# Feed-forward of a decoder layer: gate weights as the stationary operand, routes of all rows computed first, latent product ahead of the down projection

## The reference

```python
def _L0_ffn_ref(hidden_states, gate_w, up_w, down_w, fc1_w, fc2_w, expert_w, ln_gamma, ln_beta):
    HID, INT, LAT, NE, K = (512, 1024, 256, 8, 2)
    logits = jnp.einsum('bsh,he->bse', hidden_states, gate_w)
    routing_weights, selected_experts = jax.lax.top_k(logits, K)
    h = jax.nn.relu(jnp.einsum('bsh,hi->bsi', hidden_states, up_w)) ** 2
    shared_out = jnp.einsum('bsi,ih->bsh', h, down_w)
    x_latent = jnp.einsum('bsh,hl->bsl', hidden_states, fc1_w)
    expert_out = jnp.einsum('bsl,lm->bsm', x_latent, expert_w)
    moe_out = expert_out * jnp.sum(routing_weights, axis=-1, keepdims=True)
    routed_out = jnp.einsum('bsl,lh->bsh', moe_out, fc2_w)
    return _layernorm(shared_out + routed_out, ln_gamma, ln_beta)
...
x = _layernorm(x + _L0_ffn_ref(x, ...), axis=-1)
```

## Time and profile before

| | |
|---|---|
| median of 3 runs | 889.41 us (888.95 to 889.97) |
| profiled execution, its own time | 889.44 us |
| its span, first to last instruction | 887.3 us |
| PE busy | 858.8 us, 97% of the span |
| DVE busy | 608.7 us, 69% |
| POOL busy | 454.6 us, 51% |
| ACT busy | 424.6 us, 48% |
| mean granted TensorE clock | 0.995 of full speed |

### The profile page before, as it was taken

One profiled execution on the slowest core, in us unless ns is written; L12 is line 12 of the kernel. 1 busy time (PEld: TensorE's weight loads), 2 busy tenths in 40 slices (PEclk: granted clock), 3 DMA queues, 4 the chain that ended last, 5 costly groups with the idle time before them and its releaser, 6 DMA issues.

```text
span 887.3 us, 15395 instructions
## 1 busy us (share of the span) xinstructions
PE 858.8 (97%) x4780; PEld 714.8 (81%) x4780; DVE 608.7 (69%) x2043; ACT 424.6 (48%) x1430; POOL 454.6 (51%) x406
## 2 busy tenths in 40 slices
PE   7999999999999999999999999999999999999995
PEld 5787788788877788888888888888888877787884
DVE  5466788888877766666666666666667667556645
ACT  4345877777761544444444444444444455430310
POOL 4625866766674544444444444444444569471002
PEclk9999999999999999999999999999999999999998
DMA  8679998867763111213112113121131122000000
GB/s 277 263 225 214 211 184 165 184 146 159 158 233 139 39 34 35 107 37 107 37 36 108 36 37 108 36 78 66 37 107 37 48 72 85 25 11 36 13 13 35
DMA packets 68368, 88.23 MB, mean 99 GB/s; under 512 B 7232, under 2 KB 44352, under 8 KB 67264
## 3 DMA queue, kind: packets, MB, share of 16 engines
q1 hardware_dynamic: 68288, 87.26, 35.8%
HBM read 64.13 MB, written 23.07 MB: 98 GB/s over the span
## 4 chain that ended last, share of the span: by engine, by line
PE 83%; POOL 5%; DVE 4%; issue 3%; ACT 3%; DMA 1%; SPq 1%; POOLq 0%; ACTq 0%; DVEq 0%
PE banks L35 68%; PE banks L1096 6%; PE banks L1078 3%; PE banks L738 3%; PE banks L756 1%; PE banks L729 1%; POOL B_wv L171 1%; POOL x L1626 1%; PE banks L122 1%; ACT B_prob L667 1%; SPq L213 1%; POOL B_prob L579 1%; DMA heads_k<-heads_k_d 0%; DVE B_prob L824 0%; DMA stage<-xT_dram 0%
## 5 line engine op out<-in xcount | busy, mean ns | idle before, releaser
L35 PE MATMUL banks<-C_wo,C_o 128*128 128x512 f32 x768 | 192.3, 399 | 1.3 <-issue 1.2
L35 PE MATMUL banks<-xT,C_w 128*128 128x512 f32 x768 | 185.7, 390 | 0.8 <-DVE xT L137 0.8
L35 PEld LDWEIGHTS banks<-xT,C_w 128*128 128x128 f32 x768 | 143.6, 188 | 31.1 <-issue 1.6
L35 PEld LDWEIGHTS banks<-C_wo,C_o 128*128 128x128 f32 x768 | 139.6, 188 | 29.4 <-ACT C_o L1037 1.6
L1037 ACT ACTIVATE C_o<-banks 128x512 fp32r<-128x512 f32 x64 | 38.3, 598 | 231.3 <-PE banks L35 231.3
L667 ACT ACTIVATE B_prob<-B_prob,B_top 128x128 f32<-128x128 f32 x256 | 99.5, 393 | 26.4 <-DVE B_top L824 26.2
L1021 ACT ACTIVATE C_prob<-C_prob,C_top 128x128 f32<-128x128 f32 x256 | 99.0, 391 | 8.4 <-DVE C_top L1162 8.4
L171 POOL TENSOR_TENSOR C_wo<-stage,C_wo 128x512 fp32r<-128x512 f32 x32 | 40.9, 1277 | 110.6 <-ACT C_wo L166 110.6
L171 POOL TENSOR_TENSOR C_w<-stage,C_w 128x512 fp32r<-128x512 f32 x32 | 40.8, 1277 | 105.5 <-ACT C_w L166 105.4
L1224 POOL TENSOR_TENSOR C_q<-C_t,C_t 128x512 f32<-128x512 f32 x64 | 82.9, 1295 | 13.1 <-DVE C_t L1149 13.1
L579 POOL TENSOR_TENSOR B_prob<-B_prob,B_rden 128x512 f32<-128x512 f32 x64 | 67.5, 1057 | 37.0 <-DVE B_rden L833 36.6
(11 more groups left out here) (141 smaller groups left out, 1657.8 us busy)
## 6 DMA issues: line engine op xcount, KB each, us to landing
C_kv<-cross_kv_d SPq DMA_DIRECT2D x8, 1536.0 KB, 6.9
cross_kv_d<-B_v_out SPq DMA_DIRECT2D x16, 512.0 KB, 4.2
stage<-wq_dram SPq DMA_DIRECT2D x32, 256.0 KB, 2.6
stage<-wo_dram SPq DMA_DIRECT2D x32, 256.0 KB, 2.6
heads_q<-heads_q_d SPq DMA_DIRECT2D x96, 64.0 KB, 3.8
heads_k<-heads_k_d SPq DMA_DIRECT2D x96, 64.0 KB, 3.9
heads_q_d<-cT SPq DMA_DIRECT2D x8, 512.0 KB, 2.9
heads_k_d<-cT SPq DMA_DIRECT2D x8, 512.0 KB, 2.8
```

The source lines that it names most:

```text
L35: mm = eng.matmul(out, stationary[i], moving[j], start=first and n == 0, stop=last and n == len(PASSES) - 1)
```

## The change

Four edits, all in the feed-forward.

1. The gate product is turned round: `ghl` (16 or 8 columns) is stationary and the turned x moves, 512 tokens at a time, so 16 matmuls of 512 columns for all rows (`gates`), whose result has the experts on partitions. They stand on PE behind the eighth tile of half 0 (`GATES = 6`). ACT copies the two results to SBUF (`copy_gates`, in front of its work for the next tile). Behind the last tile of half 0, 8 small float32 matmuls (`turn_gates`) turn them back, 128 tokens each, and add the two parts by a 16x8 matrix of two identities (`fold`).
2. The routes of all 8 rows are made at once on DVE (`routes`), ahead of row 0.
3. Within a row, the latent product comes first; ACT copies it out, scaled by the route (`D_routed`), and z is then the down product (from PSUM) plus that.
4. In each half the order of tiles is up 0 to 5, fc1 0 and 1, up 6 and 7.

```diff
-    tiles = [("lat", l, 0) for l in range(L)] + \
-            [("up", m, 0) for m in range(M)] + [("fc1", l, 0) for l in range(L)] + \
-            [("up", m, 1) for m in range(M)] + [("fc1", l, 1) for l in range(L)]
+    GATES = 6
+
+    order = [("up", m) for m in range(6)] + [("fc1", 0), ("fc1", 1), ("up", 6), ("up", 7)]
+    tiles = [("lat", 0, 0), ("lat", 1, 0)] + [(kind, m, 0) for kind, m in order] + [(kind, m, 1) for kind, m in order]
...
+        self.gT = pool("gT", 104, [P, 2, D])
...
-        self.glo, self.logit = chip.small("D_glo", [P, self.E]), chip.small("D_logit", [P, self.E])
-        self.best, self.route = chip.small("D_best", [P, self.E]), chip.small("D_route", [P, 1])
+        self.fold, self.logit = chip.small("D_fold", [P, self.E]), chip.small("D_logit", [P, B, self.E])
+        self.best, self.route = chip.small("D_best", [P, B, self.E]), chip.small("D_route", [P, B])
...
-        self.dn, self.rt, self.gt = [chip.bank(2), chip.bank(5)], chip.bank(3), chip.bank(4)
+        self.dn, self.rt = [chip.bank(2), chip.bank(5)], chip.bank(3)
+        self.gt, self.tg = [chip.bank(4), chip.bank(3)], chip.bank(5)
...
     def scalar_rows(self, eng, b):
 
-        eng.wait_ge(self.s_gt, b + 1)
-        wait(eng, self.s_logit, b)
-        eng.activation(self.glo[:, :], self.gt[:, self.E:2 * self.E], ACT.Copy).then_inc(self.s_gcopy, 1)
-        eng.wait_ge(self.s_dn, b + 1)
+        eng.wait_ge(self.s_rt, b + 1)
+        eng.wait_ge(self.s_route, 1)
         wait(eng, self.s_z, b)
-        eng.activation(self.shared[:, :], self.dn[b % 2], ACT.Copy).then_inc(self.s_shared, 1)
+        eng.activation(self.routed[:, :], self.rt, ACT.Copy, scale=self.route[:, b:b + 1]).then_inc(self.s_routed, 1)
+
+    def copy_gates(self, eng):
+
+        for h in range(2):
+            eng.wait_ge(self.s_gt, h + 1)
+            eng.activation(self.gT[0:2 * self.E, h, :], self.gt[h][0:2 * self.E, :], ACT.Copy).then_inc(self.s_gcopy, 1)
...
             self.scalar_ahead(eng, begun + k)
+            if k == self.GATES:
+                self.copy_gates(eng)
             self.scalar_tile(eng, self.L + begun - self.FIRST + k)
...
+    def gates(self, eng):
+
+
+        eng.wait_ge(self.s_glo, 1)
+        eng.wait_ge(self.rows.s_lo, B)
+        eng.wait_ge(self.before.s_add, self.before.NS)
+        eng.wait_ge(self.before.s_olo, self.before.NS)
+        for h in range(2):
+            for c in range(C):
+                x = [self.rows.xT[:, 4 * h:4 * h + 4, lo, c, :] for lo in range(2)]
+                eng.matmul(self.gt[h][0:2 * self.E, :], self.ghl[:, c, :], x[0], start=c == 0, stop=False)
+                mm = eng.matmul(self.gt[h][0:self.E, :], self.ghl[:, c, 0:self.E], x[1], start=False, stop=c == C - 1)
+            mm.then_inc(self.s_gt, 1)
+
+    def turn_gates(self, eng):
+
+
+        eng.wait_ge(self.s_gcopy, 2)
+        eng.wait_ge(self.s_fold, 1)
+        for b in range(B):
+            mm = eng.matmul(self.tg[:, b * self.E:(b + 1) * self.E], self.gT[0:2 * self.E, b // 4, b % 4 * S:(b % 4 + 1) * S],
+                            self.fold[0:2 * self.E, :], start=True, stop=True)
+        mm.then_inc(self.s_tg, 1)
+
     def tensor_rows(self, eng, b):
 
-        h, here, n = b // 4, slice(b % 4 * S, (b % 4 + 1) * S), 2 * self.E
-        wait(eng, self.s_logit, b)
-        if b == 0:
-            eng.wait_ge(self.s_glo, 1)
-            eng.wait_ge(self.before.s_add, self.before.NS)
-        for c in range(C):
-            x = [self.rows.xT[:, b, lo, c, :] for lo in range(2)]
-            eng.matmul(self.gt[:, 0:n], x[0], self.ghl[:, c, :], start=c == 0, stop=False)
-            mm = eng.matmul(self.gt[:, 0:self.E], x[1], self.ghl[:, c, 0:self.E], start=False, stop=c == C - 1)
-        mm.then_inc(self.s_gt, 1)
-        wait(eng, self.s_shared, b - 1)
+        h, here = b // 4, slice(b % 4 * S, (b % 4 + 1) * S)
+        wait(eng, self.s_routed, b)
+        eng.wait_ge(self.s_tlo, self.number["fc1", self.L - 1, h] + 1)
+        for l in range(self.L):
+            mm = product(eng, self.rt, [t[:, here] for t in self.hT[self.M + l]], [t[:, :] for t in self.wlat[l]],
+                         l == 0, l == self.L - 1)
+        mm.then_inc(self.s_rt, 1)
+        wait(eng, self.s_z, b - 1)
+        if b == 1:
+            eng.wait_ge(self.s_logit, 1)
         for m in range(self.M):
...
-        wait(eng, self.s_z, b)
-        eng.wait_ge(self.s_tlo, self.number["fc1", self.L - 1, h] + 1)
-        for l in range(self.L):
-            mm = product(eng, self.rt, [t[:, here] for t in self.hT[self.M + l]], [t[:, :] for t in self.wlat[l]],
-                         l == 0, l == self.L - 1)
         mm.then_inc(self.s_dn, 1)
...
         for k in range(self.MT - (begun - self.FIRST)):
+            if k == self.GATES:
+                self.gates(eng)
             self.tile(eng, self.L + begun - self.FIRST + k)
             if begun + k < self.TURN + B:
                 self.turn(eng, begun + k - self.TURN)
+        self.turn_gates(eng)
         for b in range(4):
             self.tensor_rows(eng, b)
...
+    def routes(self, eng):
+
+
+        eng.wait_ge(self.s_tg, 1)
+        eng.tensor_copy(self.logit[:, :, :], self.tg[:, 0:B * self.E].rearrange("p (b e) -> p b e", e=self.E))\
+           .then_inc(self.s_logit, 1)
+        eng.wait_ge(self.s_logit, 1)
+        for b in range(B):
+            eng.max(self.best[:, b, :], self.logit[:, b, :]).then_inc(self.s_best, 1)
+        eng.wait_ge(self.s_best, B)
+        eng.tensor_tensor(self.route[:, :], self.best[:, :, 0], self.best[:, :, 1], ALU.add).then_inc(self.s_route, 1)
+
     def vector_rows(self, eng, b):
 
-        eng.wait_ge(self.s_gcopy, b + 1)
-        eng.tensor_tensor(self.logit[:, :], self.gt[:, 0:self.E], self.glo[:, :], ALU.add).then_inc(self.s_logit, 1)
-        eng.wait_ge(self.s_logit, b + 1)
-        eng.max(self.best[:, :], self.logit[:, :]).then_inc(self.s_best, 1)
-        eng.wait_ge(self.s_best, b + 1)
-        eng.tensor_tensor(self.route[:, :], self.best[:, 0:1], self.best[:, 1:2], ALU.add).then_inc(self.s_route, 1)
-        eng.wait_ge(self.s_route, b + 1)
-        eng.wait_ge(self.s_shared, b + 1)
+        eng.wait_ge(self.s_routed, b + 1)
+        eng.wait_ge(self.s_dn, b + 1)
         wait(eng, self.s_gamma, b)
         z, zg, row, gamma = self.z[:, :], self.zg, self.x2[:, b, :], self.gamma[:, :]
-        eng.scalar_tensor_tensor(out=z, in0=self.rt, scalar=self.route[:, 0:1], in1=self.shared[:, :],
-                                 op0=ALU.mult, op1=ALU.add).then_inc(self.s_z, 1)
+        eng.tensor_tensor(z, self.dn[b % 2], self.routed[:, :], ALU.add).then_inc(self.s_z, 1)
...
+        self.tile_lo(eng, self.L + self.MT - 1)
+        self.routes(eng)
         for b in range(4):
             self.vector_rows(eng, b)
         for i in range(self.L + self.MT, len(self.tiles)):
             self.vector_tile(eng, i)
+        self.tile_lo(eng, len(self.tiles) - 1)
         for b in range(4, B):
             self.vector_rows(eng, b)
```

More of the change, by code:

```diff
@@ L1270, in __init__ @@
         self.gamma, self.beta = pool("gamma", 112, [P, D]), pool("beta", 114, [P, D])
-        self.shared, self.z = pool("shared", 116, [P, D]), pool("z", 118, [P, D])
+        self.routed, self.z = pool("routed", 116, [P, D]), pool("z", 118, [P, D])
+        self.gT = pool("gT", 104, [P, 2, D])
         self.gate, self.ghl = chip.small("D_gate", [P, C * self.E]), chip.small("D_ghl", [P, C, 2 * self.E], F32R)
-        self.glo, self.logit = chip.small("D_glo", [P, self.E]), chip.small("D_logit", [P, self.E])
-        self.best, self.route = chip.small("D_best", [P, self.E]), chip.small("D_route", [P, 1])
+        self.fold, self.logit = chip.small("D_fold", [P, self.E]), chip.small("D_logit", [P, B, self.E])
+        self.best, self.route = chip.small("D_best", [P, B, self.E]), chip.small("D_route", [P, B])
         self.stats, self.moments = chip.small("D_stats", [P, 6]), chip.small("D_moments", [P, 2])
@@ L1283, in __init__ @@
         self.s_acc, self.s_pos, self.s_sq, self.s_thi, self.s_tlo = sem("acc"), sem("pos"), sem("sq"), sem("thi"), sem("tlo")
-        self.s_gt, self.s_gcopy, self.s_logit = sem("gt"), sem("gcopy"), sem("logit")
+        self.s_gt, self.s_gcopy, self.s_fold = sem("gt"), sem("gcopy"), sem("fold")
+        self.s_tg, self.s_logit = sem("tg"), sem("logit")
         self.s_best, self.s_route = sem("best"), sem("route")
-        self.s_dn, self.s_shared, self.s_z, self.s_gamma = sem("dn"), sem("shared"), sem("z"), sem("gamma")
+        self.s_rt, self.s_routed = sem("rt"), sem("routed")
+        self.s_dn, self.s_z, self.s_gamma = sem("dn"), sem("z"), sem("gamma")
         self.s_beta, self.s_res, self.s_ln2, self.s_out = sem("beta"), sem("res"), sem("ln2"), sem("out")
@@ L1296, in rank, with behind @@
         return sum(t[0] == "up" for t in self.tiles[:i + 1])
+    def behind(self, i):
+        return self.is_up(i - 1) and self.tiles[i - 1][2] == self.tiles[i][2]
     def bank(self, i):
```

(18 more changed lines are left out.)

## The result

The changed kernel takes 883.18 us (median of 6 runs, 881.27 to 884.12) against 889.07 us for the kernel before in the same runs: ratio 0.9941, 95% interval 0.9925 to 0.9957, 0.6% faster. In a second set of runs it was 883.72 us (5 runs), ratio 0.9934, 0.9921 to 0.9948. The forecast was 884.2 us.

The account below looks back on a forecast made before the run. PE, busy for 97% of the span, was taken to bound the kernel. Terms -7.62 + 3.63 + 1.9 + 0.3 + 0.4 - 1.41 - 1.68 - 0.74 = -5.2 took 889.44 to 884.2 us; range 882.8 to 887.4.

Parts of the forecast that it names:

- Gate matmuls out of the rows: PE's feed-forward rows: removing 64 gate matmuls saves 0.95 us in each of 8 rows, -7.62 us.
- New gate product: PE in half 0: 16 added gate matmuls of 512 columns at the tiles' pace, 0.2267 us each, +3.63 us.
- The rival at plain float32's pace: New gate matmuls run at plain float32's pace, 12.9 us instead of 3.63, 893.5 us in all; chance 0.05.
- Turning: PE ahead of row 0: 16 float32 records at 0.11 us plus 0.14 for lat's first weight, +1.9 us.
- Changes of tiling: PE around both new products: four places of switching the array's tiling at 0.09 us, one under a wait, +0.3 us.
- The rival with a full drain at each place: PE's tiling changes each drain the array, 1.4 us instead of 0.3, 885.3 us in all; chance 0.06.
- Wait for the gate weights: PE ahead of the new gates waits for DVE's lo part of their weights, +0.4 us, upper bound 1.3.
- Gap and half clock: Row 2: PE's wait for DVE goes, -1.41 us, and the half-clock stretch behind it, -1.68 us.
- The slack at half 1's fourth tile: DVE's first square of half 1 is done 0.9 us before PE's fourth tile needs it, so no gap there.
- The end: Last z starts right behind PE's last matmul without ACT's copy between, as a plain addition from PSUM, -0.74 us.
- this case: The main forecast for the whole kernel, 884.2 us, reaching from 882.8 to 885.6; chance 0.58.
- The half clock at the thin matmuls: Rival: clock halves behind the new gates or turning, 1.68 us each time, 885.9 or 887.6 us; chance 0.17.

Follow-up runs that it names:

- the transposes: Changed kernel with the 8 turning matmuls replaced by 8 transposes of 16 x 128, DVE adding one half: 881.98 us, ratio to before 0.9923.
- turn_k128: Changed kernel with turning matmuls over all 128 partitions of the copied gate product instead of 16: 884.83 us in one execution.
- pool_only: Kernel before with only POOL's order changed, each row's beta addition directly ahead of that row's two roots: 887.53 us, ratio 0.9985.
- gates_only: Changed kernel without the latent product first: down ahead of it, ACT copies the down product: 883.89 us, ratio 0.9941.
- old_order: Changed kernel with the tiles of a half back in the order up 0 to 7, fc1 0 and 1: 886.88 us, ratio 0.9982.
- pool_late3: Changed kernel with three more 128x512 additions on POOL between the additions of beta and the first root: 887.18 us, one execution.
- pool_late1: Changed kernel with one more 128x512 addition on POOL between the additions of beta and the first root: 882.33 us, one execution.
- gates_x4: Changed kernel with the 16 gate matmuls made four times in a row, extra results unused: 895.26 us, one execution.
- turn_x4: Changed kernel with the 8 turning matmuls made four times in a row, 64 records: 894.71 us, one execution.
- spread_x4: Changed kernel with 32 turning matmuls in eight places of 4, full matmuls between: 891.76 us, one execution.

## Why the prediction was right

The forecast was 5.2 us less; it was 5.55 by the traces and 5.9 by the medians. By its steps:

1. *Gate matmuls out of the rows, -7.62.* Rows of 6.80 us instead of 7.75: right, the whole 0.95 was theirs, the exposed weight of down included.
2. *New gate product, +3.63.* 3.71. The narrow stationary operand runs at the tiles' pace; the rival at plain float32's pace, 12.9, is out.
3. *Turning, +1.9.* 1.88, and 0.13 for lat's first weight: 2.01. The record's price, told as 0.11, is 0.112 from start to start; that it is due to 128 weight columns was not enough, as the transposes show. The Trainium skill's rule (TensorE: Matmul & The Clock Gate, LDWEIGHTS), columns and not partitions, agrees with `turn_k128` as to partitions: 0.112 a record at 128 and at 16.
4. *Changes of tiling, +0.3.* About 0.3 by the traces, but not spread over four places as I had it: all of it stands at the turning, 0.18 at its two ends and 0.13 in the tiles ahead of it. Between the gates and up 6 nothing shows: `turn_k128` has the same gates there and its two tiles take the plain 5.44. So the size was right partly by luck. The rival with a full drain at each place, 1.4 in all, is out.
5. *Wait for the gate weights, +0.4.* 0.07. This term was mis-sized. DVE's lo part ended when I said (777.61, which is 780.06 by the clock of the trace of before, told as 780.1), but behind it I had left 0.3 us for handing over and the weight load. The load, 0.09 us for 16 columns, and the first matmul both start at 777.66, 0.05 behind that end.
6. *Gap and half clock, -1.41 and -1.68.* Both gone. The gap's cause is shown from both sides: `pool_only` shrinks it to 0.24 us by POOL's order, `gates_only` removes it by PE's. The half clock went with it each time, but what set it off is less sure. Gaps of 1.56 (`old_order`) and 1.31 us (`pool_late3`) with full matmuls behind them brought none, so the gap's length alone doesn't decide; the 0.9 us of small gate matmuls behind it may. And there is one trace of the kernel before, so that each of its executions pays the 1.68 isn't shown. The slack at half 1's fourth tile, told as 0.9, was 1.1 us, and `pool_late1` put a wait exactly there.
7. *The end, -0.74.* -0.76.

The added terms are 5.92 where I had 6.23; that is the whole difference of 0.3 us. My range for this case, 882.8 to 885.6, doesn't follow from the bounds that I gave: those of terms 3 and 5 reach from 882.9 to 885.2, and term 4 had none. The half clock at the thin matmuls, told with chance 0.17, did not happen in either trace of the changed kernel; but behind a single turning of 16 records it did in three of eight traces (`old_order`, `pool_late3` and `gates_x4`; not in the two of the changed kernel, `gates_only`, `pool_late1` and `turn_k128`). So the rival was real, and that both traces of the changed kernel escaped it is in part luck. The wider product, which I had also suspected, kept the clock for 14.8 us in `gates_x4`. What decides in which execution it happens stays open, so some of the changed kernel's runs may carry those 1.6 us. Open, too, is a kernel with transposes whose POOL chain starts earlier: not tried.

## What to carry to other kernels

A gap's price can be more than its length: 1.25 us of idle PE with small matmuls behind it came with a half clock and cost 3.1 us in all, while 0.49 us ahead of the same matmuls, and 1.56 us ahead of full ones, cost no clock. So look at what follows a gap too. Before reordering products, look at which operand comes last (here the lo part of fc1): the reordering brought two new waits, 0.62 and 0.78 us, until the order of tiles covered them. And turn a narrow product so that its narrow side is the stationary one: 64 loads of wide weights for 16 columns each became 16 streams of 512.

## What the runs showed of the hardware

- Matmuls of 512 columns with 16 or 8 stationary columns run at 0.231 us and hold the granted clock at 1.00 for 14.8 us; records of 8 moving columns, back to back and with PE never idle, let it fall to 0.50 in `turn_x4` (begun at 789.9, fallen at 793.3). Bursts of 0.98 us between full matmuls didn't in `spread_x4`. One piece of 1.9 us was followed by a stretch at 0.50 in three of eight traces.
- From start to start a 16 x 128 transpose costs 0.062 us, a float32 matmul record of 8 columns with as many weight columns 0.112, at 16 partitions and at 128, and 0.21 at half clock.
- Going from the tiles into the turning's tiling of 16 rows and back cost about 0.3 us in all; going between the tiles and the gates' 16 or 8 stationary columns showed no cost (`turn_k128`: 5.44 us for the two tiles behind them).
- DVE's scaling of 512 columns took 1.51 us instead of 0.55 when POOL's addition of 1.29 us started 0.07 us ahead of it (`pool_only`).
